# Attention scores on eight places of the TensorE array, and an attention product that comes out transposed

## The reference

```python
def attn_layer(x, Wqkv, qs, ksc, Wo):          # 16 heads of 64
    q, k, v = split(x @ Wqkv, 3)
    q = l2norm(q) * qs ; k = l2norm(k) * ksc   # per head
    # rotary tables on q and k
    out = local_attention(q, k, v)             # windows of 32, each sees itself and the one before
    return out @ Wo

def local_attention(q, k, v):
    sim = einsum('bhwie,bhwje->bhwij', bq, bk2) * 8.0   # 32 queries x 64 keys
    attn = softmax(where(mask, -max, sim), -1)
    return einsum('bhwij,bhwje->bhwie', attn, bv2)
...
for i in range(6):
    x = attn_layer(shift_tokens(x), ...) + x
    x = ffn_layer(shift_tokens(x), ...) + x
```

## Time and profile before

| | |
|---|---|
| median of 3 runs | 2029.3 us (2027.05 to 2031.14) |
| profiled execution | 2026.88 us, span of its instructions 2024.6 us |
| busy: TensorE | 1831.5 us (90%) |
| busy: VectorE | 1591.9 us (79%) |
| busy: ScalarE | 1316.6 us (65%) |
| busy: GpSimd | 1353.8 us (67%) |
| mean granted TensorE clock | 0.972 |

### The profile page before, as it was taken

One profiled execution on the slowest core, in us unless ns is written; L12 is line 12 of the kernel. 1 busy time (PEld: TensorE's weight loads), 2 busy tenths in 40 slices (PEclk: granted clock), 3 DMA queues, 4 the chain that ended last, 5 costly groups with the idle time before them and its releaser, 6 DMA issues.

```text
span 2024.6 us, 80998 instructions
## 1 busy us (share of the span) xinstructions
PE 1831.5 (90%) x33507; PEld 1470.0 (73%) x33507; DVE 1591.9 (79%) x4082; ACT 1316.6 (65%) x2616; POOL 1353.8 (67%) x1002
## 2 busy tenths in 40 slices
PE   2667867999999999999999999999999999999984
PEld 1435435787888878877878788788778787888873
DVE  2586778998788888878887888888888878887851
ACT  2445545667776776677767777766776777777751
POOL 2173446676877777677767777776777677768752
PEclk9889989999999999999999999999999999999996
DMA  5234342111311111311213111113112131121101
GB/s 169 78 137 162 118 163 63 32 37 37 91 41 47 33 46 42 91 50 31 54 37 101 32 47 46 44 35 92 45 31 54 37 101 31 47 54 39 31 19 47
DMA packets 83099, 126.24 MB, mean 62 GB/s; under 512 B 41866, under 2 KB 55490, under 8 KB 82498
## 3 DMA queue, kind: packets, MB, share of 16 engines
q1 hardware_dynamic: 77352, 119.58, 19.8%
q10 hardware_dynamic: 5402, 1.71, 0.3%
HBM read 42.63 MB, written 25.16 MB: 33 GB/s over the span
## 4 chain that ended last, share of the span: by engine, by line
DVE 34%; PE 23%; issue 14%; ACT 11%; POOL 2%; DMA 0%; ACTq 0%; SPq 0%; POOLq 0%; DVEq 0%
DVE qk_s L1453 8%; DVE qk_c L1442 6%; DVE ssq L1465 6%; DVE bank L1409 4%; PE bank L929 3%; PE bank L1014 3%; PE bank L970 2%; DVE sdif L1419 2%; PE bank L1036 2%; PE bank L921 2%; PE bank L1053 2%; ACT prob L1166 2%; ACT qT L1149 2%; ACT sq L1177 2%; ACT f_h L1199 2%
## 5 line engine op out<-in xcount | busy, mean ns | idle before, releaser
L1274 POOL TENSOR_TENSOR qk_c<-qk_c,nrm 128x1024 f32<-128x1024 f32 x192 | 362.5, 1904 | 406.6 <-DVE nrm L131 406.6
L1322 POOL TENSOR_TENSOR qk_c<-qk_c,qk_s 128x1024 f32<-128x1024 f32 x192 | 451.7, 2373 | 8.4 <-DVE qk_s L1453 8.4
L1177 ACT ACTIVATE sq<-bank 128x512 f32<-128x512 f32 x384 | 232.8, 607 | 154.7 <-PE bank L1055 152.3
L1442 DVE TENSOR_TENSOR qk_c<-bank,rot 128x512 f32<-128x512 f32 x384 | 262.2, 683 | 66.2 <-ACT sq L1177 59.3
L1053 PE MATMUL bank<-w_hi,xT 128*128 128x512 f32 x576 | 280.4, 487 | 33.9 <-DVE qk_s L1453 26.1
L1453 DVE TENSOR_TENSOR qk_s<-bank,rot 128x512 f32<-128x512 f32 x384 | 261.0, 680 | 0.0
L1465 DVE TENSOR_REDUCE ssq<-sq 128x8 f32<-128x512 f32 x384 | 259.0, 675 | 0.0
L970 PEld LDWEIGHTS bank<-kT,qT 64*32 64x32 f32 x12288 | 181.0, 107 | 67.1 <-issue 67.0
L1055 PE MATMUL bank<-w_hi,xT 128*128 128x512 f32 x576 | 229.3, 398 | 0.0
L1054 PE MATMUL bank<-w_lo,xT 128*128 128x512 f32 x576 | 227.9, 396 | 0.0
L1014 PEld LDWEIGHTS bank<-v_back,pT 64*32 64x32 f32 x6144 | 187.6, 106 | 49.7 <-issue 49.4
(11 more groups left out here) (153 smaller groups left out, 3902.6 us busy)
## 6 DMA issues: line engine op xcount, KB each, us to landing
v_back<-v_own SPq DMA_DIRECT2D x96, 384.0 KB, 3.8
front_raw<-in_L_ffn_Wqkv_dram SPq DMA_DIRECT2D x18, 512.0 KB, 6.1
w_high<-front_high SPq DMA_DIRECT2D x18, 512.0 KB, 2.7
w_low<-front_low SPq DMA_DIRECT2D x18, 512.0 KB, 3.6
w_hi<-w_high SPq DMA_DIRECT2D x18, 512.0 KB, 3.8
w_lo<-w_low SPq DMA_DIRECT2D x18, 512.0 KB, 5.4
v_back<-v_own SPq DMA_DIRECT2D x72, 128.0 KB, 2.3
wo<-in_L_ffn_Wo_dram SPq DMA_DIRECT2D x6, 512.0 KB, 6.2
```

What stands on the lines that cost most here:

```text
L1177: act.activation(sq[:, n % 2, :], bank[n % 2][:, :], ACT.Square).then_inc(s["sqr"], 1)
L1274: pool.tensor_tensor(x, x, bcast(nrm[:, q.par(-1), HEADS * kind:HEADS * (kind + 1)], 2, DH), ALU.mult).then_inc(s["qkn"], 1)
L1322: pool.tensor_tensor(x, x, qk_s[:, kind, :], ALU.add).then_inc(s["rotd"], 1)
L1442: dve.tensor_tensor(qk_c[:, q.par(0), kind, 512 * half:512 * half + 512].rearrange("p (h d) -> p h d", d=DH), bank[n % 2][:, :].rearrange( ...
```

## The change

`scores` is one burst of 64 matmuls on eight places: the head of the pair (`hp`) still sets the rows of the array, but the columns now come from the parity of the pair and of the window, and each row group writes to its own bank (4 or 5). It waits for both halves of what the two bursts waited for, and stands where the first burst stood, ahead of `project(q, 3)`. `attend` is one burst, too, with the operands exchanged: 64 columns of values are stationary and 32 columns of transposed probabilities stream, so the result is the transposed output. It goes to banks 6 and 4, one for each half of the windows, and waits for both copies of the probabilities and, since it writes bank 4 from the start, for the first `score_sub` of the step. `transpose_att`, the buffer `att` and two ScalarE copies are gone; `store_attT` copies from the product's banks straight into `attT`.

```diff
-            def scores(q, half):
+            def scores(q):
...
-                b = bank[4 + half]
-                if half == 0:
-                    need(pe, s["av_r"], q.count(2, -4, 2))
-                else:
-                    need(pe, s["dif"], q.count(2, -3, 2))
-                pe.wait_ge(s["qkT_r"], q.count(4, -2, 3 + half))
+                need(pe, s["av_r"], q.count(2, -4, 2))
+                need(pe, s["dif"], q.count(2, -3, 2))
+                pe.wait_ge(s["qkT_r"], q.count(4, -2, 4))
                 j = q.idx(-2)
                 pe.nop(nofuse=True)
                 for c in range(4):
-                    pair = 4 * half + c
-                    for w in range(4):
-                        for hp in range(2):
-                            half_w, wpar = w // 2, w % 2
-                            r = slice(64 * hp, 64 * hp + 64)
-                            o = 64 * hp + 32 * wpar
-                            last = pe.matmul(
-                                b[o:o + 32, P * c + 64 * half_w:P * c + 64 * half_w + 64],
-                                qT[r, pair, WIN * w:WIN * w + WIN],
-                                kT[r, pair, P * j + WIN * w:P * j + WIN * w + 64],
-                                start=True, stop=True)
-                last.then_inc(s["sc"], 1)
+                    for half_w in range(2):
+                        for par in range(2):
+                            for wpar in range(2):
+                                for hp in range(2):
+                                    pair, w = 2 * c + par, 2 * half_w + wpar
+                                    r = slice(64 * hp, 64 * hp + 64)
+                                    o = 64 * par + WIN * wpar
+                                    last = pe.matmul(
+                                        bank[4 + hp][o:o + WIN, P * c + 64 * half_w:P * c + 64 * half_w + 64],
+                                        qT[r, pair, WIN * w:WIN * w + WIN],
+                                        kT[r, pair, P * j + WIN * w:P * j + WIN * w + 64],
+                                        start=True, stop=True)
+                last.then_inc(s["sc"], 2)
...
+            def attend(q):
...
+                need(pe, s["av_r"], q.count(2, -4, 2))
+                if roots(q):
+                    pe.wait_ge(s["nr"], q.count(1, -1, 1))
+                if q.on(-2):
+                    pe.wait_ge(s["dif"], q.count(2, -2, 1))
+                pe.wait_ge(s["pT_r"], q.count(2, -3, 2))
...
+                for pair in range(PAIRS):
+                    for wpar in range(2):
+                        for half_w in range(2):
+                            for hp in range(2):
+                                r = slice(64 * half_w, 64 * half_w + 64)
+                                v = (v_own if wpar else v_back)[r, j, DH * (2 * pair + hp):DH * (2 * pair + hp + 1)]
+                                last = pe.matmul(
+                                    bank[6 - 2 * half_w][64 * hp:64 * hp + 64, 64 * pair + WIN * wpar:64 * pair + WIN * wpar + WIN],
+                                    v, pT[r, 4 * hp + pair // 2, 64 * (pair % 2) + WIN * wpar:64 * (pair % 2) + WIN * wpar + WIN],
+                                    start=True, stop=True)
...
+            def store_attT(q, half_w):
+                act.wait_ge(s["av"], q.count(1, -3, 1))
+                need(act, s["wo_p"], q.count(1, -4, 1))
+                act.copy(attT[:, :, 64 * half_w:64 * half_w + 64],
+                         bank[6 - 2 * half_w][:, :].rearrange("p (c t) -> p c t", t=64)).then_inc(s["av_r"], 1)
...
                     if q.on(-3):
-                        store_att(q, 0)
+                        store_attT(q, 0)
+                        store_attT(q, 1)
                     ffn_place(q, 4)
                     if q.on(1):
                         squares(q.next(), 0)
-                    if q.on(-3):
-                        store_att(q, 1)
-                    if q.on(1):
                         squares(q.next(), 1)
```

More of the change, by code:

```diff
@@ L701, in stack @@
     pT = sb("pT", [P, PAIRS, P])
-    att = sb("att", [P, INNER])
     attT = sb("attT", [P, PAIRS, P])
@@ L1006, in attend @@
                 j = q.idx(-3)
[L1007 to L1028 removed]
+                for pair in range(PAIRS):
[8 more added lines that the diff above has]
+                                    start=True, stop=True)
+                last.then_inc(s["av"], 1)
             def out_proj(q):
                 shared_bank("added", q.count(1, -4, 1))
[L1032 removed]
+                pe.wait_ge(s["av_r"], q.count(2, -4, 2))
                 if q.j == 0:
@@ L1099, in body @@
                     if q.on(-3):
-                        attend(q, 0)
+                        attend(q)
                     ffn_place(q, 4)
@@ L1149, in store_qkT @@
                 act.copy(dst, src).then_inc(s["qkT_r"], 1)
-            def store_attT(q, half):
-                act.wait_ge(s["aT_p"], q.count(2, -4, half + 1))
-                need(act, s["wo_p"], q.count(1, -5, 1))
-                act.copy(attT[:, 4 * half:4 * half + 4, :].rearrange("p c t -> p (c t)"),
-                         bank[2 + half][:, :]).then_inc(s["aT_r"], 1)
             def store_probT(q, half):
                 act.wait_ge(s["pT_p"], q.count(2, -3, half + 1))
-                need(act, s["av"], q.count(2, -4, 2))
+                need(act, s["av"], q.count(1, -4, 1))
                 act.copy(pT[:, 4 * half:4 * half + 4, :].rearrange("p c t -> p (c t)"),
@@ L1167, in exponentials @@
                                ACT.Exp).then_inc(s["ex"], 1)
-            def store_att(q, half):
-                act.wait_ge(s["av"], q.count(2, -3, half + 1))
-                need(act, s["aT_p"], q.count(2, -4, half + 1))
-                act.copy(att[:, 512 * half:512 * half + 512], bank[6 if half == 0 else 4][:, :]).then_inc(s["av_r"], 1)
+            def store_attT(q, half_w):
[3 more added lines that the diff above has]
+                         bank[6 - 2 * half_w][:, :].rearrange("p (c t) -> p c t", t=64)).then_inc(s["av_r"], 1)
             def squares(q, n):
```

63 lines of the change are left out of this document (8 added, 55 removed).

## The result

The changed kernel takes **2116.2 us** (median of 4, 2111.66 to 2120.88) against 2029.1 for the one before: ratio 1.0423, 95% interval [1.0405, 1.0441]. It is 87 us slower. I had forecast 10 us faster.

A forecast was written before the change was run, and what follows sets the result against it. Bound: VectorE and ScalarE copies in j = 1 and 2, TensorE then GpSimd in j = 3. Rounds -8.8, first five steps +2.4, last full round +1.2, drain -5: -10.2 from 2029.3, 2019 us; range 2000 to 2034.

The forecast's parts named there:

- The step that failed: Score burst on TensorE: 128 records on eight places take the 1.03 us of one burst, saving 1.03 us per step.
- The attention product: TensorE's attention product takes 2.0 us in one burst; the eight transposes (0.87 us) and ScalarE's two copies of them go.
- cover, not path: TensorE's work in steps j = 1 and j = 2 isn't on the path, so savings there are worth nothing.
- ScalarE's order: Both copies now precede both squares, so the first `cos_part` of j = 1, 2, 3 comes 0.29, 0.77, 1.25 us later.
- The round: One call of `body`, four steps, gets 0.42 us shorter, to 68.8 us; 21 rounds give -8.8 us.
- `w2` is released by GpSimd: End of j = 3: TensorE arrives earlier but `w2` waits for GpSimd's last `ffn_product`, ending at about 1176.9.
- The drain: Last steps, no projection covering: 2.3 us saved in each of two steps, about 0.5 more later, -5 us.
- 1: Rival: the places don't carry; scores no faster or attention product loads and streams in turn; about 2031 to 2033 us; 20 in 100.
- 2: Rival: the order on ScalarE costs nothing and GpSimd isn't late; round gains 1.67 us, 1989 us; 15 in 100.
- 3: Rival: TensorE idles, its granted clock falls, 1.1 us added a round; slower, 2042 us; 7 in 100.
- the 4 in 100: Chance left for times outside the forecast's own case and all three rivals.
- a product over 2.6 us: Sign of being wrong: the attention product on TensorE taking over 2.6 us, where near 2.0 us was expected.

The follow-up runs named there:

- f1: Changed kernel with both bursts as 64 records of twice the columns instead of 128, some work left out so only time is read: 2031.7 us, ratio 1.0000.
- g4: f1 with attention records twice as wide again, 128 columns, values not the reference's, only time read: 2030.6 us, ratio 0.9997 against the kernel before.
- g1: Changed kernel with 143 always-met waits added to TensorE's program in each round from round 3: 2386.8 us, ratio 1.1743 against the kernel before.
- g2: g1 with 142 more always-met waits once, in round 3, moving later instruction boundaries: 2485.9 us, ratio 1.2233 against the kernel before.
- e1: Kernel before with only the changed scores, 128 records on eight places in one burst, and its own attention product: 2031.9 us, ratio 1.0011.
- e9: Kernel before with only its scores put on eight places, still two bursts of 64 around projection 3: 2022.8 us, ratio 0.9964.
- e4: Changed kernel with its scores cut into two bursts of 64 around projection 3: 2077.5 us, ratio 1.0227 against the kernel before.
- e5: Changed kernel with scores cut in two around projection 3 and attention product around projection 0, signalled once at its end: 2133.1 us, ratio 1.0496.
- h1: Changed kernel with 36 small extra matmuls as filling in each round from round 3: 2088.6 us, ratio 1.0282 against the kernel before.
- e7: Changed kernel with both bursts cut in two around projections, and ScalarE's attT stores and squares in turn: 2096.5 us, ratio 1.0314.

## Why the prediction was wrong

- **The step that failed** is "Eight starts of 7 ns fit into 56 ns. So 128 score records on eight places should take sixteen turns again". It takes a rate from eight loads and applies it to 256 instructions. Twice wrong. First, sizes: without a stall the burst lasts 1.48 us, not the 1.03 to 1.10, so the saving was 0.72 us a step (2 x 1.10 less 1.48), not 1.03. Second, and this is the loss: nothing in the sum asked where 256 instructions in 1.5 or 2.1 us come from. They come 256 at a time, and the least distance between two fetches' starts is 3.2 to 3.5 us in each of the traces but f1's and g4's, which fetch half as often (5.2 and more). The Trainium skill, "Runtime: NRT & Kernel Launch", section "Instruction fetch mechanics", has these blocks of 256 instructions, and says that the cost of crossing from one to the next is "mostly hidden", since instructions issue more slowly than they are refilled. The trace agrees on the size (253 packets, 4.15 MB) and not on the hiding: 2 stalls in the kernel before, 54 in the changed one.
- **What it is worth.** By parts of the span (85.3 us longer): 57.8 in the 80 steady steps, which is 20 rounds of +3.18 for stalls and -0.28 (within 0.5) for the rest by the fit; 27.5 at the ends. g1 against g2 puts 84 us of stalls at some 85 us, g4 puts the kernel without them at no loss in the steady steps (-5.2). How the 27.5 divide is not separated: g4's ends are 13.1 longer than before, with no stall: 3.7 ahead of the first step, 3.3 in the first 15 (forecast 2.4), 6.2 behind the last. Some of that is chance: g4's traced execution was the slowest of its ten (2034.3 for a median of 2030.6) and that of before one of the fastest (2026.9), and the 3.7 lie in code that wasn't changed.
- **The attention product** was right in size: 2.07 us for 2.0, and the transposes and copies went. Mis-priced was its place. I called TensorE's work in steps 1 and 2 "cover, not path". g4 against f1 bears that out up to 2 us; beyond it an added 2 us stall (this product is read by the copies and so by the norms) is path, by 0.6 of itself in the fit (standard error 0.16).
- **ScalarE's order** was right: from `add_ffn` on, g4's first `cos_part` of steps 1, 2 and 3 comes 0.31, 0.81 and 1.30 us later than before (medians; forecast 0.29, 0.77 and 1.25).
- **The round** without stalls: 69.03 in g4, 68.8 forecast (-0.42), measured -0.25. `w2` is released by GpSimd: in g4 it starts 0.15 us after the last `ffn_product` in 23 of 24 rounds, where before it came 1.8 us behind it in 21. That path was read rightly.
- **The drain** didn't get its 5 us shorter: in g4 it is 6 longer, of which a part may be chance, as said. There `w2` runs for 4.54 us at 1940.41, where it took 2.92 before; the granted clock was 0.57 from 1941 to 1945.
- **Rivals.** 1 is half right (the eight places bring little: e1 1.0011, e9 0.9964) and names no stall. 2 fell with g4. 3 has the right sign by the wrong means: the clock does fall behind 2 us gaps (71.7 us below 0.9 from 330 to 1990 us, against 5.9 before), but f1 had 174 us of that and g4 41, and they take the same time within 1.1 us. Its 2042 was the highest of all my cases; the measured 2116.2 lies in the 4 in 100 that I had left outside them.
- I had named a product over 2.6 us as a sign of being wrong. Its mean was 2.62, its median 2.07.

## What to carry to other kernels

Count instructions per microsecond, not only TensorE's array time: small matmuls on several places use up 256 instructions in 1.5 to 2 us, and TensorE then stops for about 2 us with "issue" as the only releaser. Let each record do more (no stall in g4). Keeping such bursts to 64 records with long matmuls between them helps less surely: 28 stalls in the scores became 17 in e4, 9 in e1 became 7 in e9, and e5 kept 33 in both bursts, though shorter ones. When you count where the boundaries fall, count what stands directly before and behind a burst as part of it (g1, h1). And when two halves become one, ask who waited for the first half: in this kernel a single signal for both, alone, cost 3%.

## What the runs showed of the hardware

- Load-and-matmul pairs of 64 rows x 32 columns on eight places go through at 11.6 ns each over a burst of 128 (1.48 us), not at the 7 ns of eight loads; on four places of 64 x 64 at 16 ns (2.07), on two at 29 ns (3.72). The Trainium skill, "TensorE: Matmul & The Clock Gate", Part 1, has back-to-back starts never below about 25 ns apart; with several places in turn the measured 11.6 and 16 ns decide against that here. Records of 128 columns took 18 ns on eight places (1.16 us for 64) and 31 ns on four, where those of 64 took 18: wide records are cheaper by the column and half as many to fetch.
- An always-met wait on TensorE costs about 0.1 us: 79 of them took 7.55 us in g2, and 143 lengthened g1's round by 15.2 us (84.2 for 69.0), of which 0.9 is the stop in the projection.
- In the changed kernel none of the 88 boundaries before record 76 of a burst stalled, and 54 of the 77 later ones did; of the 11 in scores that didn't, 9 lie in step 3, with feed-forward matmuls ahead. In bursts of 64 records stalls came as early as record 7 (e7).
